# An adaLN FFN kernel: h transposed by transfers and VectorE blocks, LoRA three tiles behind, and a reordered tail

## What is computed

```python
base = jnp.einsum('btd,od->bto', x, W)
logits = jnp.einsum('btd,ed->bte', x, Wr)
logits = logits + one_hot(language_ids, 8)[:, None, :] * 5.0
topw, topi = jax.lax.top_k(logits, 2)
weights = softmax(topw)
gates = sum(one_hot(topi, 8) * weights[..., None], axis=-2)
h = jnp.einsum('btd,erd->bter', x, A)
lora_out = jnp.einsum('bter,bte,eor->bto', h, gates, B)
cond = base + 2.0 * lora_out
out = x + jnp.einsum('bsi,io->bso', cond, sign) * softplus(scale)
```

## Time and profile before

| | us |
|---|---|
| median of 3 runs (lowest, highest) | 166.83 (166.54, 167.04) |
| the profiled execution | 166.99 |
| its span | 165.2 |
| TensorE busy in it | 159.7 (97%) |
| VectorE busy | 97.1 (59%) |
| ScalarE busy | 65.6 (40%) |
| GpSimd busy | 53.5 (32%) |

### The profile page before, as it was taken

The page is one execution under the profiler, slowest core; times in us unless marked ns, Lnnn a source line. Parts: engine busy times, 40 slices in busy tenths (PEclk is TensorE's granted clock), DMA queues, the critical chain, the costliest instruction groups (busy, mean ns, idle before and its releaser), DMA issues.

```text
span 165.2 us, 3733 instructions
## 1 busy us (share of the span) xinstructions
PE 159.7 (97%) x1082; PEld 154.5 (94%) x1082; DVE 97.1 (59%) x416; ACT 65.6 (40%) x176; POOL 53.5 (32%) x51
## 2 busy tenths in 40 slices
PE   7999997999999999999999999999999999999993
PEld 5688887999999999999999999999999999999982
DVE  5769967555555655554554555555565555555551
ACT  3444642443444333344444434434443333344240
POOL 2993665222222333333333332222223333333000
PEclk9999999999999999999999999999999999999999
DMA  5992424234333333333333333333333333111113
GB/s 168 355 175 77 122 65 126 78 101 132 125 119 116 119 125 113 126 127 127 127 127 127 126 109 101 106 122 119 115 122 124 114 126 113 63 63 65 66 65 127
DMA packets 27351, 19.51 MB, mean 118 GB/s; under 512 B 5168, under 2 KB 22352, under 8 KB 27344
## 3 DMA queue, kind: packets, MB, share of 16 engines
q1 hardware_dynamic: 26768, 18.38, 35.7%
q10 hardware_dynamic: 576, 1.05, 1.8%
HBM read 11.03 MB, written 8.39 MB: 118 GB/s over the span
## 4 chain that ended last, share of the span: by engine, by line
PE 80%; DVE 8%; DMA 4%; SPq 2%; ACT 2%; issue 1%; DVEq 0%
PE pair L626 65%; PE pair L643 13%; DMA scale_in<-in_L_ffn_scale 4%; PE p_ht L650 2%; DVE xt L436 2%; SPq L227 1%; SPq L245 1%; DVE second L534 1%; DVE wide_lo L487 1%; DVE m_full L483 1%; ACT wide_hi L375 1%; DVE top_no L529 1%; DVE b_lo L496 0%; DVE h_gated L543 0%; DVE wide_lo L476 0%
## 5 line engine op out<-in xcount | busy, mean ns | idle before, releaser
L306 POOL TENSOR_TENSOR xt_lo<-xt,xt_hi 128x512 fp32r<-128x512 f32 x32 | 41.1, 1286 | 90.0 <-ACT xt_hi L357 89.9
L626 PE MATMUL pair<-wide_hi,xt_hi 128*128 128x256 f32 (+2 forms) x260 | 63.0, 319 | 0.2 <-POOL xt_lo L306 0.2
L626 PE MATMUL pair<-wide_hi,xt_lo 128*128 128x256 f32 (+2 forms) x260 | 60.3, 310 | 0.0
L626 PE MATMUL pair<-wide_lo,xt_hi 128*128 128x256 f32 (+2 forms) x260 | 60.3, 309 | 0.0
L626 PEld LDWEIGHTS pair<-wide_hi,xt_hi 128*128 128x128 f32 x260 | 40.1, 189 | 0.8 <-POOL xt_lo L306 0.5
L626 PEld LDWEIGHTS pair<-wide_hi,xt_lo 128*128 128x128 f32 x260 | 40.3, 188 | 0.0
L626 PEld LDWEIGHTS pair<-wide_lo,xt_hi 128*128 128x128 f32 x260 | 40.2, 188 | 0.0
L401 ACT ACTIVATE y<-pair 128x256 f32<-128x256 f32 x31 | 11.9, 385 | 45.0 <-PE pair L643 45.0
L511 DVE TENSOR_TENSOR logits<-pair,bias 128x8 f32<-128x8 f32 x32 | 5.3, 165 | 35.9 <-PE pair L626 35.9
L436 DVE STREAM_TRANSPOSE xt<-x_in 128x512 f32<-128x512 f32 x32 | 22.7, 711 | 3.7 <-DVE top L519 3.2
L357 ACT ACTIVATE xt_hi<-xt 128x512 fp32r<-128x512 f32 x32 | 20.3, 634 | 2.6 <-DVE xt L436 2.6
(11 more groups left out here) (76 smaller groups left out, 134.4 us busy)
## 6 DMA issues: line engine op xcount, KB each, us to landing
x_in<-in_x SPq DMA_DIRECT2D x128, 64.0 KB, 1.9
out<-y SPq DMA_DIRECT2D x31, 256.0 KB, 2.1
sign_in<-in_L_ffn_sign ACTq DMA_DIRECT2D x4, 256.0 KB, 5.4
w_in<-in_L_cond_W SPq DMA_DIRECT2D x4, 256.0 KB, 5.2
a_in<-in_L_cond_A SPq DMA_DIRECT2D x4, 64.0 KB, 5.2
b_in<-in_L_cond_B SPq DMA_DIRECT2D x2, 128.0 KB, 4.9
out<-y SPq DMA_DIRECT2D x2, 128.0 KB, 1.8
wr_in<-in_L_cond_Wr SPq DMA_DIRECT2D x4, 4.0 KB
```

The lines of the kernel that those rows point to most:

```text
L306: nc.gpsimd.tensor_tensor(xt_lo[n][:, :, :].rearrange("p j (g b) -> p g j b", g=NQ), xt[n][:, :, :, :], xt_hi[n][:, :, :].bitcast(FP32).re ...
L626: last = nc.tensor.matmul(pair[n][bank][:, at0:at0 + hi - lo], l[:, k, :], w[:, k, lo:hi], start=(opens and k == 0 and l is xt_hi[n] and w ...
```

## The change

Everything that was a ring of three is now a ring of four (RING = 4), and the eight PSUM banks are four pairs. p_b2 takes pair[3][0] in the start, so tile 3 waits for b2_lo. LAG is 3.

For tiles 0 to 28 TensorE transposes no h. SyncE moves h_gated with four DMAs from SBUF to SBUF (`move_h`): each takes 32 of the 128 columns from all 128 partitions to 32 partitions, in pieces of 128 bytes, 4 pieces per partition. VectorE then transposes the 32x32 blocks (`turn_h`, in step t + 3), ScalarE makes ht_hi, and GpSimd (no longer VectorE) ht_lo. In this path the tokens of a column are permuted, and the two splits put them back in order.

Tiles 29 to 31 are still transposed by TensorE, to banks that have come free (p_ht is now a table), with ht_lo on VectorE.

ScalarE issues the store of tiles 0 to 28 itself, after its y copies; xt_hi moves ahead of the y copies in its order. In the tail the last two tiles run together: bank 0 of tile 30, bank 0 of tile 31, bank 1 of tile 30, bank 1 of tile 31, with the LoRA products and transposes between.

The diff, cut to its core (S3 becomes RING throughout, in lines not shown):

```diff
-    S3 = 3
+    RING = 4
...
-        h_gated = sb("h_gated", [P, ER])
+        h_gated = [sb(f"h_gated{n}", [P, ER]) for n in range(RING)]
+        h_moved = [sb(f"h_moved{n}", [P, NQ, Q]) for n in range(RING)]
+        ht = sb("ht", [ER, NQ, Q])
...
-                for n in range(S3)]
-        p_ht = ctx.enter_context(nc.psum_tensor("p_ht", [P, 512], FP32))
-        p_b2 = ctx.enter_context(nc.psum_tensor("p_b2", [P, 512], FP32))
+                for n in range(RING)]
+        p_b2 = pair[3][0]
         p_m = [pair[1][0], pair[1][1], pair[2][0], pair[2][1]]
+        p_ht = {TILES - 3: pair[(TILES - 1) % RING][1], TILES - 2: pair[(TILES - 4) % RING][0],
+                TILES - 1: pair[(TILES - 4) % RING][1]}
...
-        LAG = 2
-        FIRST = LAG + S3
-        LOOPS = (TILES - LEAD - FIRST) // S3
-        AFTER = FIRST + S3 * LOOPS
+        LAG = 3
+        LATE = TILES - 3
+        FIRST = LAG + RING
+        LOOPS = (TILES - LEAD - FIRST) // RING
+        AFTER = FIRST + RING * LOOPS
...
+            def move_h(q, r, d):
+
+                n = slot(r, d)
+                sp_eng.wait_ge(h_gated_made, RING * q + r + d + 1)
+                for i in range(NQ):
+                    sp_eng.dma_start(h_moved[n][Q * i:Q * i + Q, :, :], h_gated[n][:, Q * i:Q * i + Q])\
+                        .then_inc(h_arrived[n], 16)
+
             def turnover(q, r, s):
 
-                if s is None or s + S3 < TILES:
-                    sp_eng.wait_ge(xt_made, S3 * q + r + 1)
-                    load(q, r, S3 * q + r + S3)
-                if s is None or s >= LAG + LEAD:
+                if s is None or 0 <= s - LEAD - 1 < LATE:
+                    move_h(q, r, -LEAD - 1)
+                if s is None or s + RING < TILES:
+                    sp_eng.wait_ge(xt_made, RING * q + r + 1)
+                    load(q, r, RING * q + r + RING)
+                if s is not None and s - LAG - LEAD >= LATE:
                     store(q, r, -LAG - LEAD)
...
+            def low_h(done):
+
+                pool.wait_ge(ht_hi_made, done - LAG + 1)
+                nc.gpsimd.tensor_tensor(ht_lo[:, :].rearrange("p (b g) -> p g b", g=NQ), ht[:, :, :],
+                                        ht_hi[:, :].bitcast(FP32).rearrange("p (b g) -> p g b", g=NQ),
+                                        ALU.subtract).then_inc(ht_lo_made, 1)
+
             def step(q, r, s):
+                if s is None or 0 <= s - LAG < LATE:
+                    low_h(RING * q + r)
                 if has(s, LEAD):
                     low_x(q, r, LEAD)
...
+            def high_h(done, late):
+
+                if late is None:
+                    act.wait_ge(ht_made, done - LAG + 1)
+                    nc.scalar.activation(ht_hi[:, :].rearrange("p (b g) -> p g b", g=NQ), ht[:, :, :], ACT.Copy)\
+                        .then_inc(ht_hi_made, 1)
+                else:
+                    act.wait_ge(ht_turned, late - LATE + 1)
+                    act.wait_ge(y_summed, late)
+                    nc.scalar.activation(ht_hi[:, :], p_ht[late][:, 0:P], ACT.Copy).then_inc(ht_hi_made, 1)
+
             def step(q, r, s):
-                if has(s, -LAG):
-
-                    act.wait_ge(ht_turned, S3 * q + r - LAG + 1)
-                    nc.scalar.activation(ht_hi[:, :], p_ht[:, 0:P], ACT.Copy).then_inc(ht_hi_made, 1)
+                if s is None or 0 <= s - LAG < LATE:
+                    high_h(RING * q + r, None)
                 if has(s, -1):
 
-                    act.wait_ge(top_made, S3 * q + r)
+                    act.wait_ge(top_made, RING * q + r)
                     nc.scalar.activation(e2[:, :], top[:, 0:1], ACT.Exp, bias=top[:, 1:2], scale=-1.0)\
                         .then_inc(e2_made, 1)
+                if has(s, LEAD):
+                    high_x(q, r, LEAD, first=(s is not None and s + LEAD < RING))
+                if s in (TILES, TILES + 1):
+                    high_h(s, s - 2)
                 if has(s, -LAG):
                     n = slot(r, -LAG)
 
-                    act.wait_ge(y_summed, S3 * q + r - LAG + 1)
-                    if s is None or s - LAG >= S3:
+                    act.wait_ge(y_summed, RING * q + r - LAG + 1)
+                    if s is None or s - LAG >= RING:
                         act.wait_ge(y_stored[n], 16 * turn(q, r, -LAG))
                     if s != TILES - 1 + LAG:
                         nc.scalar.activation(y[n][:, 0:Y0], pair[n][0][:, HEAD:HEAD + Y0], ACT.Copy)
                     nc.scalar.activation(y[n][:, Y0:D], pair[n][1][:, 0:D - Y0], ACT.Copy).then_inc(y_copied, 1)
-                if has(s, LEAD):
-                    high_x(q, r, LEAD, first=(s is not None and s + LEAD < S3))
+                    if s is None or s - LAG < LATE:
+                        act.wait_ge(y_copied, RING * q + r - LAG + 1)
+                        act.dma_start(out[:, RING * q + r - LAG, :], y[n][:, :]).then_inc(y_stored[n], 16)
+                if s == TILES - 1:
+                    high_h(s, LATE)
 
             steps(act, step)
+            act.wait_ge(y_copied, TILES)
+            act.dma_start(out[:, TILES - 1, Y0:D], y[(TILES - 1) % RING][:, Y0:D])\
+                .then_inc(y_stored[(TILES - 1) % RING], 16)
...
+            def low_h(tile):
+
+                dve.wait_ge(ht_hi_made, tile + 1)
+                nc.vector.tensor_tensor(ht_lo[:, :], p_ht[tile][:, 0:P], ht_hi[:, :].bitcast(FP32), ALU.subtract)\
+                    .then_inc(late_ht_lo_made, 1)
+
+            def turn_h(q, r, s):
+
+                n = slot(r, -LAG)
+                dve.wait_ge(h_arrived[n], 16 * NQ * (turn(q, r, -LAG) + 1))
+                if s is None or s > LAG:
+                    dve.wait_ge(ht_lo_made, RING * q + r - LAG)
+                nc.vector.transpose(ht[:, :, :].rearrange("p g b -> p (g b)"),
+                                    h_moved[n][:, :, :].rearrange("p g c -> p (g c)")).then_inc(ht_made, 1)
...
-                hurry = s is not None and s >= TILES - 1
-                if has(s, -LAG) and not hurry:
-                    low_h(done)
+                if s is None or 0 <= s - LAG < LATE:
+                    turn_h(q, r, s)
+                if s == TILES:
+                    low_h(TILES - 3)
...
+                    if s == TILES:
+                        low_h(TILES - 2)
...
+                if s == TILES + 1:
+                    low_h(TILES - 1)
...
+            def turn_h(tile):
+
+                pe.wait_ge(h_gated_made, tile + 1)
+                nc.tensor.transpose(p_ht[tile][:, 0:P], h_gated[tile % RING][:, :], ident[:, :]).then_inc(ht_turned, 1)
 
             def step(q, r, s):
-                done = S3 * q + r
+                done = RING * q + r
                 if has(s, 0):
 
                     pe.wait_ge(xt_lo_made, done + 1)
-                    if s is None or s >= S3:
-                        pe.wait_ge(y_copied, done - S3 + 1)
+                    if s is None or s >= RING:
+                        pe.wait_ge(y_copied, done - RING + 1)
+                    if s == RING - 1:
+                        pe.wait_ge(b2_lo_made, 1)
                     for k in range(KC // 2):
                         m_there(s, k)
                         wide(r, [k], BANKS, opens=True)
                 if has(s, -LAG):
 
-                    if s == LAG:
-                        pe.wait_ge(b2_lo_made, 1)
                     pe.wait_ge(ht_lo_made, done - LAG + 1)
                     lora(slot(r, -LAG), (0, 1)).then_inc(y_summed, 1)
                 if has(s, 0):
                     for k in range(KC // 2, KC):
                         m_there(s, k)
                         wide(r, [k], BANKS, signals=True)
-                if has(s, -1):
-                    turn_h(done)
 
             def finish(s):
 
-
-                r, n = s % S3, s % S3
-                everything = range(KC)
+                before, r = (s - 1) % RING, s % RING
+                first, second = range(KC // 2), range(KC // 2, KC)
+
+                pe.wait_ge(xt_lo_made, s)
+                pe.wait_ge(y_copied, s - RING)
+                wide(before, first, (BANKS[0],), opens=True)
+                pe.wait_ge(ht_lo_made, s - 3)
+                lora((s - 4) % RING, (0, 1)).then_inc(y_summed, 1)
+                wide(before, second, (BANKS[0],)).then_inc(head_ready, 1)
+                pe.wait_ge(y_copied, s - RING + 1)
+                turn_h(s - 2)
+
                 pe.wait_ge(xt_lo_made, s + 1)
-                pe.wait_ge(y_copied, s - S3 + 1)
-                wide(r, everything, ((0, 0, HEAD),), opens=True).then_inc(head_ready, 1)
-                pe.wait_ge(ht_lo_made, s - LAG + 1)
-                lora(slot(r, -LAG), (0, 1)).then_inc(y_summed, 1)
-                wide(r, range(KC // 2), (BANKS[1],), opens=True)
+                wide(r, first, (BANKS[0],), opens=True)
+                pe.wait_ge(ht_lo_made, s - 2)
+                lora((s - 3) % RING, (0, 1)).then_inc(y_summed, 1)
```

(56 more changed lines are left out.)

53 lines of the change are left out of this document (22 added, 31 removed).

## The result

The changed kernel takes **181.03 us** (median of 4 runs, 180.66 to 181.28) where the kernel before took 166.89 beside it (166.54 to 167.04): a ratio of 1.083, 95% interval 1.080 to 1.087. It is 14 us slower. I had forecast 162.1 us and a range of 161.0 to 165.8; the sign was wrong, and the range missed by 15 us.

The account below looks back on a forecast made before the run. TensorE was taken as the bound, 4.38 us a tile falling to 4.27. The terms -3.3 (loop), -0.8 (start) and -0.57 (tail) sum to -4.7, so 166.83 becomes 162.1 us; range 161.0 to 165.8.

Parts of the forecast that it names:

- SyncE's queue: SyncE's eight DMA issues per tile: a turn of 4.06 to 4.21 us, under TensorE's 4.27, so cost zero.
- The rule I wrote down: Rival in which SyncE's issues become the bound from a mean spacing of 0.534 us: 165.6 us in all, chance 0.13.
- The move's landing: Moves of h_gated inside SBUF: landing takes 1.9 us, so h arrives 2.3 us early and costs nothing.
- Rival 2: Moves of h land late, at 4.9 us: 4.60 us a tile, 171 us in all, chance 0.08.
- rival 4: The change removes less: the transpose's 0.114 us on TensorE was partly cover for a wait for ht_lo; chance 0.02.
- From arrival to LoRA: Chain from logits over transpose, ht_hi and ht_lo: ends 1.34 us after tile start, wanted at 1.67, slack 0.3, no stall.
- Rival 3: The h chain through GpSimd takes 0.4 us more than counted: 0.1 a tile, +2.7, 164.8 us, chance 0.08.
- GpSimd's race with the gate: GpSimd's xt_lo against VectorE's gate, within 0.05 us: lost, h_gated is up to 1.2 late, absorbed, so zero.
- ScalarE's queue: ScalarE with xt_hi ahead of the y copies and the store behind: copies end near S + 3.5, S being tile start; cost zero.
- Part 1's gain: Loop, tiles 0 to 28: 29 transposes leave TensorE at 0.114 us each, -3.3 us, 4.27 a tile.
- Part 3: Tail: the last two tiles run as whole halves, -0.57 us; waits sum to 0.64, no change.
- Part 2, the start: First tiles: TensorE's stall of 1.03 us goes, a new one of about 0.2 comes, -0.8 us.

Follow-up runs that it names:

- e7: The changed kernel with SyncE's turns written out one by one instead of a hardware loop: 178.22 us, ratio 1.066.
- e10: The changed kernel, but the four moves per tile read their pieces from x in device memory instead of h_gated: 168.43 us, ratio 1.008.
- e9: The changed kernel, all eight issues still on SyncE, but VectorE transposes h at the end of the step before: 179.67 us, ratio 1.078.
- e2: The changed kernel, but x is loaded by two transfers of 128 KB per tile instead of four of 64: 171.86 us, ratio 1.025.
- e4: As e3, but VectorE transposes h at the end of the step before, with a small operation between logits and maximum: 164.04 us, ratio 0.981.
- e3: The changed kernel with full work, but two of the four x loads per tile are issued by ScalarE: 167.68 us, ratio 1.002.
- e8: As e4, but with SyncE's turns written out instead of a hardware loop: 163.72 us, ratio 0.980.

## Why the prediction was wrong, point by point

**SyncE's queue: the step that failed.** The term was 3 x 0.475 + 0.55 for the moves and 3 x 0.50 + 0.58 for the loads, 4.06 to 4.21, against TensorE's 4.27. The loads were right (1.95 where they had 2.08). The moves take 2.75 where they had 2.0: three spacings of 0.63, and 0.87 from the last move to the first load. I had priced a kind of transfer that no row showed with the row of another kind, and called a cover of 0.06 to 0.2 "the thinnest" without widening the bound by what that kind might cost. The rule I wrote down, "begins at a mean spacing of 0.534", was right: the mean is 4.70 / 8 = 0.59.

How 4.70 becomes the loss: the 23 turns from 32.79 to 146.53 take 4.945 on average. 4.70 is the floor, 0.1 is the loop's return, and most of the rest lies in two turns of 6.03 and 5.66 us, in which four loads took 3.20 and 2.84 to issue. The first of them:

```profile
37.75 2.49 SPq L270 DMA_DIRECT2D h_moved<-h_gated  x4
40.53 3.20 SPq L234 DMA_DIRECT2D x_in<-in_x  x4
43.66 0.31 DVE L554 STREAM_TRANSPOSE ht<-h_moved 128x128 f32<-128x128 f32 x1 [2.81 <-DMA h_moved<-h_gated]
43.78 2.50 SPq L270 DMA_DIRECT2D h_moved<-h_gated  x4
45.09 0.30 PEld L698 LDWEIGHTS pair<-b_hi,ht_hi 128*128 128x128 f32 x2 [2.81 <-POOL ht_lo L347]
```

Such a turn stands near 40 us in e7 (6.14) and e10 (6.51) as well; what lengthens it is open. The second one, behind the loop's first return, stands in e9 (5.54), e10 (5.55) and e2 (5.76), and is gone in e7, where SyncE has no loop. With the slack of e4 neither costs anything.

**The account.** Span forecast 160.5, measured 179.0. First LoRA product 33.41 instead of 32.35: +1.1. From there to the product of tile 27 131.66; the forecast gives 26 x 4.27, and for the last distance, in the tail, 3.56 and a wait of 0.29, so 114.9: +16.8. The later waits in the tail 1.00 instead of 0.35: +0.65. Together 18.5 of 18.5.

**The move's landing**: right. 1.9 forecast, 1.8 measured; the 4.9 of b_in wasn't the pieces of 128 bytes by themselves. Rival 2 is out, and rival 4 by e4, where a tile is 4.28 instead of 4.38. The Trainium skill's "DMA: Bandwidth & Descriptors", "Why small descriptors are slow (HBM only)", exempts transfers inside SBUF. The 1.8 us agree with that but don't test it, since e10's moves, the same pieces out of device memory, landed in 1.8 us too.

**From arrival to LoRA**: three links were priced too short. Here is the chain of one tile, the longest of four:

```profile
92.58 0.17 DVE L563 TENSOR_TENSOR logits<-pair,bias 128x8 f32<-128x8 f32 x1 [1.48 <-PE pair L681]
92.95 0.31 DVE L554 STREAM_TRANSPOSE ht<-h_moved 128x128 f32<-128x128 f32 x1 [0.20 <-DVE logits L563]
93.30 0.43 ACT L412 ACTIVATE ht_hi<-ht 128x128 fp32r<-128x128 f32 x1 [1.71 <-DVE ht L554]
93.80 0.53 POOL L347 TENSOR_TENSOR ht_lo<-ht,ht_hi 128x128 fp32r<-128x128 f32 x1 [1.99 <-ACT ht_hi L412]
94.39 0.30 PEld L698 LDWEIGHTS pair<-b_hi,ht_hi 128*128 128x128 f32 x2 [0.21 <-POOL ht_lo L347]
```

Transpose 0.31 (I had 0.27), ht_hi 0.43 (0.28), ht_lo 0.53 (0.40). Logits to transpose is 0.37 in this tile, 0.29 in the next, and 0.20, as I had it, in the other two of four. So the chain from the logits' start to the product is 1.81, 1.73, 1.64 and 1.64, on average 1.70 instead of 1.26. The prediction wants the product 1.67 after a tile's start and has the logits start at 0.08, so 1.59 were there. The slack of 0.3 was gone, and 0.22, 0.14, 0.05 and 0.05 are missing: added to 4.28 they give the 4.51, 4.42, 4.32 and 4.32 of e3. The pattern has the period of the loops (four steps); that VectorE's loop return makes it wasn't tried. Rival 3 was true too, at 0.11 a tile (e3 less e4), as priced; I had given it a chance of 0.08.

**GpSimd's race with the gate**: it didn't cost. gate started at 94.93, xt_lo at 95.06, and none of the 32 gate operations took over 0.23. **ScalarE's queue**: right, no wait of TensorE for a copy.

**Part 1's gain**: right, once its covers held: 4.28 in e4 and e8. **Part 3**: e4's waits for the LoRA products of tiles 27, 28 and 29 are 0, 0.29 and 0.22, where the prediction had 0.29, 0.18 and 0.17. In the change they are 0.80, 0.80 and 0.20, since the longer chain has only six matmuls as cover there. The -0.57 was right within 0.1: without the waits, e8 needs 13.43 us from the product of tile 26 to its last matmul; the kernel before, from that of tile 27, 13.51, and one LoRA product more (0.71), one transpose less (0.11) and the -0.57 make 13.54 of it.

**Part 2, the start**: wrong. A stall of 1.03 gone and 0.2 new was the sum; in the change the new one is 1.10, and in e8 still 1.18. The release was as counted (28.09 against 27.97); four issues take 1.9 to the last and not 1.43, VectorE's transpose starts at 31.97 and not 31.3, and the chain behind it takes 1.44 and not 1.0. So the start brings nothing. e8's first LoRA product is at 33.69 instead of 32.35, which is most of the 1.6 us between e8's 163.7 and the forecast of 162.1.

In sum: the size of the removed work was right to 0.01 us a tile. The two terms that cover it were too small, and the measured ones are 4.70 against 4.06 for the queue's turn (16% more) and 1.70 against 1.26 for the chain (35% more).

## What to carry to other kernels

- When work leaves the engine that is the bound by way of a DMA, add up the issuing queue's turn as carefully as the engine's, and price each issue by its kind (source, destination, size). If no row shows the kind, its bound must reach over the slack; a cover of 0.06 us in 4.27 is none.
- A queue that issues back to back shows in the page's chain (as SPq here) and in a timeline as rows without gaps. Moving two issues to a queue that has room was worth 13 us here, more than everything that the change aimed at.
- When one bound is mended and the time only comes back to where it was, look for the second before judging the idea: e3 is no faster than before, and e4 is, by 1.9%.
